# The last stage of a transformer block on one core: another split of the sums, roots and normalisations among the engines

## Reference, cut to what matters

```python
def _layernorm(x, axis=-1, eps=1e-05):
    m = jnp.mean(x, axis=axis, keepdims=True)
    v = jnp.var(x, axis=axis, keepdims=True)
    return (x - m) / jnp.sqrt(v + eps)
...
    x = x + _layernorm(_L0_attn_ref(_layernorm(x, axis=-1), ...), axis=-1)
    x = x + _layernorm(_L0_ffn_ref(_layernorm(x, axis=-1), ...), axis=-1)
    return x
```

## Time and profile before

| | before |
|---|---|
| median of 3 runs | 594.15 us (593.56 to 595.57) |
| profiled execution, its own time | 596.54 us |
| its span in the profile | 594.8 us |
| busy share of the span | TensorE 89%, ScalarE 67%, VectorE 63%, GpSimd 59% |
| the last `put` is issued | 562.59 us |
| the first load of the last stage is issued | 565.73 us |
| last store issued | 591.46 us |

### The profile page before, as it was taken

The page is one execution under the profiler, slowest core; times in us unless marked ns, Lnnn a source line. Parts: engine busy times, 40 slices in busy tenths (PEclk is TensorE's granted clock), DMA queues, the critical chain, the costliest instruction groups (busy, mean ns, idle before and its releaser), DMA issues.

```text
span 594.8 us, 14582 instructions
## 1 busy us (share of the span) xinstructions
PE 529.3 (89%) x4947; PEld 387.8 (65%) x4947; DVE 376.3 (63%) x1087; ACT 396.9 (67%) x884; POOL 348.5 (59%) x453
## 2 busy tenths in 40 slices
PE   6989899999899899998899899999886699999980
PEld 4655456556566446655555666889886699999930
DVE  6824583965975946996947786637752365555247
ACT  3488989888978788859788786644542355555425
POOL 6103636545538885357877358488678755465534
PEclk9999999999999999999999999999997899999986
DMA  7346323213214322222734511212222213321174
GB/s 196 77 128 160 111 93 110 71 46 108 80 37 130 103 76 82 76 96 79 203 104 139 137 56 46 65 51 64 56 64 66 65 34 90 83 67 33 33 283 142
DMA packets 47016, 55.62 MB, mean 94 GB/s; under 512 B 7376, under 2 KB 41056, under 8 KB 44784
## 3 DMA queue, kind: packets, MB, share of 16 engines
q1 hardware_dynamic: 42624, 45.76, 27.0%
q0 software_dynamic: 4320, 8.92, 4.6%
HBM read 36.27 MB, written 18.92 MB: 93 GB/s over the span
## 4 chain that ended last, share of the span: by engine, by line
PE 56%; DVE 15%; ACT 9%; POOL 6%; issue 5%; another core or an unknown queue 4%; DMA 3%; DVEq 1%; SPq 0%; ACTq 0%; POOLq 0%
PE SC L862 11%; PE OA L739 9%; PE OA L872 6%; PE M L777 4%; PE M L813 4%; PE SC L721 3%; ACT arena L1006 3%; PE SC L725 2%; PE M L634 2%; DVE SS L1322 2%; PE SC L731 2%; PE M L653 2%; POOL slots L1752 1%; PE M L843 1%
## 5 line engine op out<-in xcount | busy, mean ns | idle before, releaser
L1006 ACT ACTIVATE arena<-SC 128x1024 f32<-128x1024 f32 x160 | 161.9, 1038 | 14.6 <-PE SC L726 11.8
L862 PE MATMUL SC<-arena 128*128 128x128 f32 (+1 forms) x852 | 108.9, 279 | 0.0
L862 PEld LDWEIGHTS SC<-arena 128*128 128x128 f32 (+1 forms) x852 | 101.6, 187 | 0.4 <-issue 0.3
L739 PE MATMUL OA<-arena 128*32 128x256 f32 (+1 forms) x1536 | 88.9, 349 | 6.6 <-DVE arena L446 2.8
L1752 POOL DMA_INDIRECT slots<-XBA,IDX x64 | 72.8, 1138 | 37.0 <-DVE IDX L1447 19.6
L1495 DVE TENSOR_TENSOR arena<-arena,SC 128x256 f32<-128x256 f32 (+1 forms) x142 | 43.6, 348 | 64.0 <-issue 22.3
L872 PE MATMUL OA<-arena 128*128 (+1 forms) x426 | 62.0, 283 | 13.5 <-issue 7.6
L739 PEld LDWEIGHTS OA<-arena 128*32 128x32 f32 x1536 | 39.3, 109 | 44.0 <-issue 22.9
L872 PEld LDWEIGHTS OA<-arena 128*128 128x128 f32 (+1 forms) x426 | 54.4, 195 | 16.2 <-issue 16.2
L445 POOL TENSOR_TENSOR arena<-arena 128x512 f32<-128x512 f32 x32 | 42.7, 1335 | 36.2 <-ACT arena L1006 35.6
L438 POOL TENSOR_TENSOR arena<-arena 128x512 f32<-128x512 f32 x23 | 31.2, 1356 | 48.9 <-ACT arena L1006 48.9
(11 more groups left out here) (254 smaller groups left out, 1086.1 us busy)
## 6 DMA issues: line engine op xcount, KB each, us to landing
arena<-parts SPq DMA_DIRECT2D x90, 192.0 KB
parts<-arena SPq DMA_DIRECT2D x16, 384.0 KB, 3.0
arena<-ytok SPq DMA_DIRECT2D x8, 512.0 KB, 6.6
XGA<-slots SPq DMA_DIRECT2D x39, 65.0 KB
arena<-slots SPq DMA_DIRECT2D x32, 65.0 KB
X<-in_L_attn_x SPq DMA_DIRECT2D x4, 512.0 KB, 5.2
out<-X SPq DMA_DIRECT2D x8, 256.0 KB, 2.4
arena<-parts SPq DMA_DIRECT2D x12, 96.0 KB
```

The lines of the kernel that those rows point to most:

```text
L739: mm = pe.matmul(OA[32 * j:32 * j + 32, q0:q0 + n], vals[:, t, 32 * h:32 * h + 32], probs(j), start=first, stop=last, skip_group_check=True)
L862: mm = pe.matmul(SC[0:n, r % 2, 512 * m + P * c:512 * m + P * (c + 1)], WSEL[s % 4][:, I * m + i0:I * m + i0 + n], XGT[r % 2], start=True, ...
L1006: act.activation(EB[u], SC[:, n % 2, :], ACT.Exp).then_inc(exp_done, 1)
```

## The change

It redistributes the work of the last stage; nothing before it differs.

- Sums: GpSimd adds batches 0, 1, 2, 3 and 5, all in a row at the head of its part of the stage; TensorE sums 4, 6 and 7; VectorE none.
- The filler ahead of TensorE's sums grows from 14 to 40 matmuls.
- Roots: VectorE makes those of pairs 0 and 3 (semaphore `f_dve_rstd`), GpSimd those of pairs 1 and 2 (`f_rstd`).
- Normalisations: VectorE does batches 5 and 7 (`f_dve_ln`), ScalarE does 1, 0, 3, 2, 4, 6 in that order.
- Residuals: GpSimd adds 1, 3, 2, 4, 7, VectorE 0, 5, 6; the stores go out as 0, 1, 3, 2, 4, 5, 7, 6.
- `moments` is cut in two, `stats_of` and `moments`, with a semaphore `f_bn` between them, so that other work can stand between the two halves.

```diff
-        BY_POOL, BY_VECTOR = (1, 4), (7,)
-        BY_TENSOR = [b for b in range(NB) if b not in BY_POOL + BY_VECTOR]
-        OUT_POOL, OUT_VECTOR = (0, 1, 2, 4), (3, 7, 5, 6)
+        BY_POOL, BY_TENSOR = (0, 1, 2, 3, 5), (4, 6, 7)
+        ROOT_POOL, ROOT_VECTOR = (1, 2), (0, 3)
+        NORM_SCALAR, NORM_VECTOR = (1, 0, 3, 2, 4, 6), (5, 7)
+        OUT_POOL, OUT_VECTOR = (1, 3, 2, 4, 7), (0, 5, 6)
...
-            for b in (0, 1, 3, 2, 4, 7, 5, 6):
+            for b in (0, 1, 3, 2, 4, 5, 7, 6):
                 store(sp, b)
...
-            keep_busy(14)
+            keep_busy(40)
             for b in BY_TENSOR:
                 pe.wait_ge(yt_in[b], 16)
...
             final_seeds(0)
+            final_norm(1)
+            final_seeds(1)
             final_norm(0)
-            final_seeds(1)
-            final_norm(1)
-            final_norm(2)
             final_seeds(2)
             final_norm(3)
+            final_norm(2)
+            final_seeds(3)
             final_norm(4)
-            final_seeds(3)
-            final_norm(5)
             final_norm(6)
...
+            stats_of(0)
+            moments(0)
+            stats_of(1)
+            moments(1)
+            stats_of(2)
+            final_root(0)
+            stats_of(3)
+            moments(2)
+            moments(3)
+            stats_of(4)
+            stats_of(5)
+            moments(4)
+            moments(5)
+            residual(0)
+            stats_of(6)
+            stats_of(7)
+            moments(6)
+            moments(7)
+            norm(5)
+            final_root(3)
+            norm(7)
+            residual(5)
+            residual(6)
...
-            add_pair(BY_POOL[0])
-            final_root(0)
-            add_pair(BY_POOL[1])
+            for b in BY_POOL:
+                add_pair(b)
             final_root(1)
-            residual(OUT_POOL[0])
+            residual(1)
             final_root(2)
-            for b in OUT_POOL[1:]:
-                residual(b)
+            residual(3)
+            residual(2)
+            residual(4)
+            residual(7)
```

More of the change, by code:

```diff
@@ L312, in block_kernel @@
         f_out = [sem("f_out0"), sem("f_out1")]
-        f_seed, f_sum = sem("f_seed"), sem("f_sum")
+        f_seed, f_sum, f_bn = sem("f_seed"), sem("f_sum"), sem("f_bn")
+        f_dve_rstd, f_dve_ln = sem("f_dve_rstd"), sem("f_dve_ln")
         out_done = [sem("out_done0"), sem("out_done1")]
@@ L391, in summed, with rooted @@
             return SUMS[b][:, P * t:P * (t + 1)] if b in BY_TENSOR else FY[b][:, 0, t, :]
+        def rooted(eng, b):
+            if b // 2 in ROOT_POOL:
+                eng.wait_ge(f_rstd, ROOT_POOL.index(b // 2) + 1)
+            else:
+                eng.wait_ge(f_dve_rstd, ROOT_VECTOR.index(b // 2) + 1)
         NBLK = E * I // P
@@ L1226, in final_norm @@
             def final_norm(b):
-                act.wait_ge(f_rstd, b // 2 + 1)
+                rooted(act, b)
                 for t in range(T):
@@ L1623, in _, with stats_of @@
                 step(s, s % RING)
[L1627 to L1638, removed]
+            def stats_of(b):
                 if b in BY_TENSOR:
                     dve.wait_ge(sum_full, BY_TENSOR.index(b) + 1)
-                elif b in BY_POOL:
+                else:
                     dve.wait_ge(f_sum, BY_POOL.index(b) + 1)
@@ L1645, in moments @@
                     last = dve.bn_stats(ST[:, T * b + t, :], summed(b, t))
-                link(last)
+                last.then_inc(f_bn, 1)
+            def moments(b):
+                dve.wait_ge(f_bn, b + 1)
                 for t in range(T):
@@ L1649, in moments @@
                 last.then_inc(f_stat, 1)
[L1651 to L1674, removed]
-                residual(b)
+            def final_root(q):
+                pair = slice(2 * T * q, 2 * T * (q + 1))
+                y, a, u = RSR[:, 0, pair], NWC[:, 0:2 * T], NWA[:, 0:2 * T]
+                dve.wait_ge(f_stat, 2 * q + 2)
+                link(dve.tensor_scalar(a, MV[:, pair, 1], LN_EPS, None, ALU.add))
+                dve.wait_ge(f_seed, 2 * q + 2)
+                link(dve.tensor_tensor(u, y, y, ALU.mult))
+                link(dve.scalar_tensor_tensor(u, u, -0.5, a, ALU.mult, ALU.mult))
+                link(dve.scalar_tensor_tensor(y, u, 1.5, y, ALU.add, ALU.mult))
+                dve.scalar_tensor_tensor(NM0[:, 0, pair], MV[:, pair, 0], -1.0, y, ALU.mult, ALU.mult).then_inc(f_dve_rstd, 1)
@@ new lines, in norm, with residual @@
+            def norm(b):
+                rooted(dve, b)
+                for t in range(T):
+                    i = T * b + t
+                    last = dve.tensor_scalar(FY[b][:, 0, t, :], summed(b, t), MV[:, i, 0:1], RSR[:, 0, i:i + 1],
+                                             ALU.subtract, ALU.mult)
+                last.then_inc(f_dve_ln, 1)
+            def residual(b):
+                if b in NORM_VECTOR:
+                    dve.wait_ge(f_dve_ln, NORM_VECTOR.index(b) + 1)
+                else:
+                    dve.wait_ge(f_ln, NORM_SCALAR.index(b) + 1)
+                x1 = X[:, T * b:T * (b + 1), :]
+                dve.tensor_tensor(x1, x1, FY[b][:, 0], ALU.add).then_inc(f_out[0], 1)
@@ L1807, in _ @@
                 put(s, s % RING)
[L1809 to L1813, removed]
             def add_pair(b):
@@ L1818, in add_pair, with residual @@
                 pool.tensor_tensor(FY[b][:, 0], FY[b][:, 0], FY[b][:, 1], ALU.add).then_inc(f_sum, 1)
+            def residual(b):
+                if b in NORM_VECTOR:
+                    pool.wait_ge(f_dve_ln, NORM_VECTOR.index(b) + 1)
+                else:
+                    pool.wait_ge(f_ln, NORM_SCALAR.index(b) + 1)
+                x1 = X[:, T * b:T * (b + 1), :]
+                pool.tensor_tensor(x1, x1, FY[b][:, 0], ALU.add).then_inc(f_out[1], 1)
             def final_root(q):
```

## The result

The changed kernel is slower. Over 22 runs of each, the medians are 599.48 us (595.44 to 602.51) after and 595.74 us (590.96 to 600.55) before; the ratio is 1.0081 with a 95% interval of 1.006 to 1.0102. That is +4.8 us (3.6 to 6.1), where +1.7 us was forecast; the two medians alone differ by 3.7 us. A later comparison on one chip gave 1.0112 (1.0063 to 1.0162).

A forecast was written before the change was run, and what follows sets the result against it. The prediction took VectorE's unbroken work to bound the stage's end. Last residual +1.7 us, adding-up correction +0.2 and stores -0.2 gave +1.7: median 594.15 to 595.8 us, with an 8-in-10 range of 593.9 to 597.3.

The forecast's parts named there:

- The filler holds the sums, VectorE idles: Before TensorE's sums: 40 matmuls take 17.2 us, batch 4's sum starts 3.9 us late, VectorE idles 3.5 us.
- The early part is worth nothing: GpSimd's sums of the first batches: VectorE some 1 us ahead, lost in the later gap, so costed at nothing.
- Meetings with GpSimd's adds: VectorE's normalisation of batch 5 and last root wait for GpSimd's residual adds; root ends at 589.75 instead of 588.5.
- Rival 1: Tail: fewer meetings of VectorE with GpSimd's adds, +0.8 down to -0.4 us, 594.9 to 593.8 us; chance 0.15.
- The tail to the last residual: Last normalisations and residuals: the last residual ends at 593.15 instead of 591.44, +1.7 us.
- From the last residual to the end: Stores behind the last residual: their gaps and last landing change the end by -0.2 us.
- the term for the stores: End of the stage: gaps between the last stores of 1.1 and 0.55 us, usual landing 2.4 us; -0.2 us.
- The sum: Whole last stage: +1.7 us, median 594.15 to 595.8 us.
- Rival 2 (clock): TensorE's clock falls under the filler, all three sums come 1.7 us later; +3.4 us, 597.5 us; chance 0.11.
- Rival 3: Filler is over by 574.5, sums come as batches land; -0.6 to -4.0 us, 593.5 to 590.2 us; chance 0.11.

## Why the prediction was wrong, point by point

- *The filler holds the sums, VectorE idles.* Right: the first sum started at F + 17.3 at a clock of 1.00 (17.2 forecast), VectorE idled for 3.75 us (3.5 forecast), the eighth `f_stat` was 0.9 us late (0.9 forecast). Shown by the two runs that change the filler alone.
- *The early part is worth nothing.* Right: all of it lies ahead of that idle time.
- *Meetings with GpSimd's adds.* Right in place and size: 2.7 us for the normalisation of batch 5 (587.95 - 585.3 = 2.65 forecast) and one add in front of the third instruction of the root. L1660 took 1.14 us beside the add of 586.43, so an instruction with two SBUF inputs of this kind does wait. The trace agrees with the rule of the Trainium skill ("SBUF — State Buffer", Who interferes with whom) that the prediction cites. Rival 1 is out.
- *The tail to the last residual.* +1.7 forecast, +1.9 with the 0.2 us by which the adding up came out early, and +2.2 measured. The root ended 0.15 us later than forecast, and the normalisation of batch 7 out of PSUM took 1.37 us, where 1.1 was taken within bounds of 1.0 and 1.4. The order of the last adds was another one: VectorE's two went first (1.29 us together), and GpSimd's residual 7 lasted 2.24 us behind them and was the last, where the forecast had it ahead of residual 6. In time up to the last residual that order costs under 0.1 us.
- *From the last residual to the end.* This step failed. The prediction took the 3.4 us of the kernel before, less 0.2 for the stores, as if only stores stood behind the last residual; it measured 5.15 us, +1.8 where -0.2 was forecast. The drain of GpSimd's queue stands there too, with 5.15 us from GpSimd's last instruction to the end of the span. In the kernel before it was hidden, with 1.8 us to spare, because GpSimd's last residual ended at 587.86 and VectorE's at 591.44. The change gave GpSimd the residual of batch 7, which became the last one to end. The drain cost 1.5 us and was among neither the terms nor the rivals; the term for the stores was +0.3 in place of -0.2, because the residual of batch 7 ended last and the store of batch 6 stands behind its store. That the drain is the cause is shown by the added memset (+2.0 between the last residual and the end, with the stores unchanged) and by moving residual 7 away (-1.5 by the drain, -2.3 in all). The order of the last adds does not excuse the step: with the forecast's own end of GpSimd's residual 7, 592.6, the drain would have ended the program at 592.6 + 5.15 = 597.75, which is +3.0 and not +1.7.
- *The sum.* Last residual +2.2, end +1.8, together 4.0 us in the stage, against 1.7 forecast and 4.8 (3.6 to 6.1) measured. Whether the 0.8 us between is more than chance stays open; the profiles show nothing of it in the stage, and the medians of the runs differ by 3.7 us only.
- *Rival 2 (clock).* Out: the granted clock was 1.00 throughout the filler. *Rival 3.* Out: the 40 matmuls took the 17.3 us that the rows of before gave, not 13.3.

## What to carry to other kernels

Look at what stands behind the last instruction of every engine, not only behind the last store: an engine whose share of the page is small can own the end of the program. Give the last work to the engine that leaves its block fastest, and see that GpSimd is done some 5 us before the end of the program; here that means at least 1.8 us before VectorE's last residual. A filler that keeps TensorE's clock up should end just before the work that it prepares; beyond that, each matmul is a delay of the whole queue. And where instructions of two engines wait for each other, as VectorE's and GpSimd's do here, moving an instruction forward can move the meeting to the next one: in these runs the time went by the number of long adds met, two or three, and not by which instruction met them.

## What the runs showed of the hardware

- GpSimd's end of program is long: in all fourteen profiles, a DRAIN of its queue ended 4.90 to 4.92 us after its last instruction, be that an add of 1.26 us or a memset of 0.2 us. Where nothing else was later, the span ended 0.23 us after it, and in none earlier. The DRAIN of VectorE's queue ended 0.05 us after VectorE's last instruction in all fourteen, that of ScalarE's 0.04 us.
- VectorE's turns against GpSimd's adds went one by one: four 128x128 instructions beside three adds took 3.73 us, three small ones took 0.87, 1.18 and 1.19 us, each behind one add.
- With all eight loads issued in one go, the third and all behind it landed about 1 us late in two of fourteen profiles; in one pair of profiles of the same kernel (32.1 and 33.3 us) the stage moved by as much.
